# Rows of maxima stored to DRAM in one transfer and loaded in three; queries, features and a value projection of a pass dealt out one step later

## The reference, cut to what matters

```python
mod = (silu(c) @ wmod).reshape(8, 6, 1, 256)          # sa, ca, ga, sb, cb, gb
h = layernorm(x) * (1 + ca) + sa
x = x + ga * attention0(h)      # 16 heads of 16, causal, softmax
h = layernorm(x) * (1 + cb) + sb
x = x + gb * ffn(h)
# ffn(h): xn = layernorm(h) * ln_g + ln_b; o = attention1(xn) + h   (32 heads of 8, not causal)
#         y = gelu(o @ w1[e] + b1[e]) @ w2[e] + b2[e]   with 8 experts, 256 tokens each, chosen by position
```

## Time and profile before

| | |
|---|---|
| median of 3 runs | 1596.53 us (1594.93 to 1596.89) |
| profiled execution | 1600.5 us, its span 1598.7 us |
| TensorE (PE) | busy 1428.8 us, 89% |
| DVE / ACT / POOL | busy 1148.2 us (72%) / 997.1 us (62%) / 485.3 us (30%) |
| mean granted TensorE clock | 0.962 |
| DMA | 203.32 MB, mean 127 GB/s |
| store_max L1016 / load_max L1026 | 288 / 192 issues |
| chain that ended last | PE 65%, DVE 10%, ACT 7%, SPq 6%, DMA 6% |

### The profile page before, as it was taken

One profiled execution on the slowest core, in us unless ns is written; L12 is line 12 of the kernel. 1 busy time (PEld: TensorE's weight loads), 2 busy tenths in 40 slices (PEclk: granted clock), 3 DMA queues, 4 the chain that ended last, 5 costly groups with the idle time before them and its releaser, 6 DMA issues.

```text
span 1598.7 us, 29723 instructions
## 1 busy us (share of the span) xinstructions
PE 1428.8 (89%) x9541; PEld 601.4 (38%) x9541; DVE 1148.2 (72%) x2891; ACT 997.1 (62%) x2075; POOL 485.3 (30%) x1219
## 2 busy tenths in 40 slices
PE   6676578998999989999999989999999989998987
PEld 4222323333344434343343434343343423343426
DVE  6654579868879686878778686878778597867620
ACT  1143256775677766676577766686577766776761
POOL 4122233434333243413333143413233033201000
PEclk9698799999999999999999999999999999999999
DMA  6841434564438273546438263555437342524212
GB/s 189 219 109 29 142 88 112 155 162 130 113 103 232 73 206 88 161 119 181 100 96 234 78 199 95 144 136 169 112 95 203 96 113 72 160 79 106 81 43 66
DMA packets 192734, 203.32 MB, mean 127 GB/s; under 512 B 58048, under 2 KB 143360, under 8 KB 192584
## 3 DMA queue, kind: packets, MB, share of 16 engines
q1 hardware_dynamic: 186696, 197.05, 44.9%
q10 hardware_dynamic: 5888, 4.37, 1.0%
HBM read 123.43 MB, written 77.94 MB: 126 GB/s over the span
## 4 chain that ended last, share of the span: by engine, by line
PE 65%; DVE 10%; ACT 7%; SPq 6%; DMA 6%; issue 4%; POOL 1%; POOLq 0%; ACTq 0%; DVEq 0%
PE bank_out L1471 16%; PE bank_scores L1452 12%; PE bank_max L1430 8%; PE bank_side L1555 7%; PE bank_side L1394 5%; PE bank_side L1404 4%; DVE max_column L1699 3%; PE bank_max L1539 3%; ACT probs L1252 3%; DMA max_rows<-max_parts 2%; PE bank_side L1520 2%; PE bank_side L1509 2%; PE bank_side L1539 2%; SPq L944 2%; SPq L829 2%
## 5 line engine op out<-in xcount | busy, mean ns | idle before, releaser
L1252 ACT ACTIVATE probs<-bank_scores 128x512 f32<-128x512 f32 (+3 forms) x1536 | 752.4, 543 | 333.0 <-PE bank_scores L1452 323.7
L1699 DVE TENSOR_REDUCE max_column<-bank_max 128x1 f32<-128x512 f32 x1024 | 654.3, 684 | 121.8 <-PE bank_max L1430 116.3
L1452 PE MATMUL bank_scores<-q_stack,k_stack 64*128 64x512 bf16 (+3 forms) x2048 | 321.0, 350 | 62.0 <-ACT probs L1252 36.7
L1471 PE MATMUL bank_out<-probs,v_tile 128*9 128x512 f32 (+4 forms) x3072 | 368.4, 552 | 7.8 <-POOL probs L1120 2.9
L1430 PE MATMUL bank_max<-k_stack,q_stack 64*128 64x512 bf16 (+3 forms) x2048 | 319.7, 349 | 49.0 <-DVE max_column L1696 19.1
L1696 DVE CUSTOM_DVE_ANT_0 bank_max<-bank_max,causal 128x384 f32<-128x384 f32 (+3 forms) x512 | 241.7, 515 | 131.2 <-PE bank_max L1430 128.9
L1452 PEld LDWEIGHTS bank_scores<-q_stack,k_stack 64*128 64x128 bf16 x2048 | 81.5, 94 | 442.2 <-issue 409.3
L1102 POOL CAST max_parts<-max_row 128x32 bf16<-128x32 f32 x96 | 23.2, 241 | 456.4 <-DVE max_row L1712 456.4
L1430 PEld LDWEIGHTS bank_max<-k_stack,q_stack 64*128 64x128 bf16 x2048 | 104.2, 95 | 126.7 <-issue 87.0
L1555 PE MATMUL bank_side<-w_out,hidden_T 128*128 128x256 f32 x512 | 141.5, 402 | 3.1 <-issue 1.1
L1120 POOL TENSOR_SCALAR_AFFINE_SELECT probs<-probs 128x512 f32<-128x512 f32 x128 | 81.4, 636 | 97.8 <-ACT probs L1252 97.5
(11 more groups left out here) (153 smaller groups left out, 1361.2 us busy)
## 6 DMA issues: line engine op xcount, KB each, us to landing
q_stack<-q_parts SPq DMA_DIRECT2D x124, 256.0 KB, 4.6
k_stack<-k_parts SPq DMA_DIRECT2D x122, 192.0 KB, 6.2
out_raw<-out_raw SPq DMA_DIRECT2D x70, 256.0 KB, 2.0
w_in<-in_L_ffn_w_dram SPq DMA_DIRECT2D x16, 1024.0 KB, 7.0
w_out<-in_L_ffn_w_dram SPq DMA_DIRECT2D x16, 1024.0 KB, 6.3
q_parts<-partsq SPq DMA_DIRECT2D x32, 384.0 KB, 3.1
k_parts<-partsk SPq DMA_DIRECT2D x32, 384.0 KB, 2.9
q_parts<-partsq SPq DMA_DIRECT2D x32, 256.0 KB, 3.2
```

Source lines behind the costliest of these rows:

```text
L1252: nc.scalar.activation(probs[s % 2][:, head_at(k), q0:S], region[bank][:, q0:S], ACT.Exp, scale=float(WIDTH[a]) ** -0.5).then_inc(drained[ ...
L1452: ins = pe.matmul(region[to][:, q0:S], k_stack[buf][rows, at, kt * P:(kt + 1) * P], q_stack[buf][rows, at, q0:S], start=(i == 0), stop=last)
L1471: ins = pe.matmul(outb[32 * k:32 * k + WIDTH[a] + 1, q0:S], v_tile[a][:, kt, g * GROUP + k, :], probs[s % 2][:, k, q0:S], start=(kt == 0), ...
L1699: v.tensor_reduce(dst, region[bank], AX_X, ALU.max).then_inc(drained[bank], 1)
```

## The change

`max_rows` in DRAM gets another layout, so that the store is a single transfer of 128 rows of 192 bytes, and the load is one transfer for each bf16 part, over both halves of the partitions, whose pieces in DRAM are 64 bytes long (before, two transfers with three rows each). The semaphores' counts follow. `store_max` gets slot 1 instead of 2 of its count, which is slot 2 instead of 3 of the step: the same half, but ahead of what stands in slot 3. In each pass one value projection goes from 61 to 33 and the four attention outputs to 41, 43, 53, 61; the second half of the features, the eight halves of queries and keys, four pieces of the expert output, and store_y, load_expert_out and load_gate go one step later (features 341 and 343 become 343 and 353).

```diff
@@ -50,7 +50,7 @@
 VALUES_SLOT = (3, 1)
 ROWS_AFTER = 1
 BLOCK = 32
-MAX_HOPS = (("max_rows", 0), ("store_max", 2), ("load_max", 4))
+MAX_HOPS = (("max_rows", 0), ("store_max", 1), ("load_max", 4))
 NORMALISE_AFTER = 3
 TURN_SLOT = 1
 NEWTON_PIECE = 3 + GUESS_STEPS
@@ -287,10 +287,10 @@
 
 
     b, e = n + 1, n - 1
-    place_units(plan, first, (3, 13, 61, 63), v_items(0, n + 2))
+    place_units(plan, first, (3, 13, 33, 63), v_items(0, n + 2))
     place_units(plan, first, (13,), [("bias_part", n, 0)])
     place_units(plan, first, (23,), [("head_features", b, 0, 1)])
-    place_units(plan, first, (33, 41, 43, 53), out_items(b))
+    place_units(plan, first, (41, 43, 53, 61), out_items(b))
     place_units(plan, first, (191, 231, 231, 243, 281), heads_items(n, 1, 0))
     place_units(plan, first, (271, 301, 301, 321, 351), heads_items(n + 2, 0, 0))
     place_units(plan, first, (421, 441, 441, 463, 491), heads_items(n, 1, 1))
@@ -318,11 +318,11 @@
     place_cluster(plan, first, 303, e, 1, norm_under(n + 3, 0) if more else ())
     place_units(plan, first, (341,), [("load_expert_in", n, 0)])
     if more:
-        place_units(plan, first, (341, 343), features_items(n + 3, 0))
-        place_units(plan, first, (393, 403, 411, 421, 431, 441, 451, 461), qk_items(0, n + 3))
+        place_units(plan, first, (343, 353), features_items(n + 3, 0))
+        place_units(plan, first, (403, 411, 421, 431, 441, 451, 461, 471), qk_items(0, n + 3))
     place_expert_out(plan, first, (311, 313, 323, 333), e, 1, 0)
-    place_expert_out(plan, first, (353, 363, 373, 383), e, 1, 1)
-    place_units(plan, first, (402, 413, 423), [("store_y", e, 1), ("load_expert_out", n, 0), ("load_gate", n + 1)])
+    place_expert_out(plan, first, (363, 373, 383, 393), e, 1, 1)
+    place_units(plan, first, (412, 423, 433), [("store_y", e, 1), ("load_expert_out", n, 0), ("load_gate", n + 1)])
     place_units(plan, first, (413,), [("keep_v", n + 1)])
     place_units(plan, first, (471,), [("bias_columns", n)])
 
@@ -554,7 +554,7 @@
               nc.dram_tensor("k_parts1", (2, C, SLICES, P, S), BF16, kind="Internal").ap()]
     raw_dram = [nc.dram_tensor("out_raw%d" % a, (HEADS[a] // GROUP, P, S), F32, kind="Internal").ap() for a in range(2)]
     inverse_dram = [nc.dram_tensor("inverse%d" % a, (C, HEADS[a] // C, S), F32, kind="Internal").ap() for a in range(2)]
-    max_dram = nc.dram_tensor("max_rows", (2, M_PARTS, BLOCK, P // BLOCK, BLOCK), BF16, kind="Internal").ap()
+    max_dram = nc.dram_tensor("max_rows", (2, P // BLOCK, BLOCK, M_PARTS, BLOCK), BF16, kind="Internal").ap()
     mod_dram = nc.dram_tensor("mod_rows", (BATCHES, 4 * D), F32, kind="Internal").ap()
 
     with ExitStack() as ctx:
@@ -758,11 +758,11 @@
 
         def rows_sent(b, a, g):
 
-            return 16 * M_PARTS * (HEADS[a] // GROUP // 2 * b + g // 2 + 1)
+            return 16 * (HEADS[a] // GROUP // 2 * b + g // 2 + 1)
 
         def rows_stored(b, a, g):
 
-            return 16 * TILES * (HEADS[a] // GROUP // 2 * b + g // 2 + 1)
+            return M_PARTS * rows_sent(b, a, g)
 
         def chunk_of(a, g):
 
@@ -1011,19 +1011,17 @@
                 ago = groups_ago(b, a, g, 2)
                 if ago:
                     wait(sp, max_stored[ago[1]][g % 2], rows_stored(*ago))
-                for m in range(M_PARTS):
-                    dst = max_dram[g % 2, m].rearrange("c q j -> q c j")
-                    sp.dma_start(dst, max_parts[:, g % 2, m, :]).then_inc(max_sent[a][g % 2], 16)
+                dst = max_dram[g % 2].rearrange("q c m j -> (q c) (m j)")
+                sp.dma_start(dst, max_parts[:, g % 2, :, :].rearrange("p m j -> p (m j)")).then_inc(max_sent[a][g % 2], 16)
 
             def load_max(b, f, a, g):
                 u = unit_of(a, g * GROUP)
                 per, at = GROUP // TILES, column_of(a, g, PASSES[a] - 1, 0)
                 wait(sp, max_sent[a][g % 2], rows_sent(b, a, g))
-                for t in range(TILES):
-                    first = MAX_ROW + t * TILE_ROWS
-                    dst = q_stack[buffer_of(u, b)][first:first + M_PARTS, at:at + per, :]
-                    src = max_dram[g % 2][:, t * per * T:(t + 1) * per * T].rearrange("m (k c) q j -> m k (c q j)", k=per)
-                    sp.dma_start(dst, src).then_inc(max_stored[a][g % 2], 16)
+                for m in range(M_PARTS):
+                    dst = q_stack[buffer_of(u, b)][MAX_ROW + m:P:TILE_ROWS, at:at + per, :]
+                    src = max_dram[g % 2, :, 0:GROUP * T, m, :].rearrange("q c j -> c q j")
+                    sp.dma_start(dst.rearrange("p h (t x) -> p (h t) x", t=T), src).then_inc(max_stored[a][g % 2], 16)
 
             def store_y(b, f, j):
                 wait(sp, y_made, 2 * b + j + 2)
```

## The result

| | median | runs | ratio to the kernel before, 95% interval |
|---|---|---|---|
| before | 1596.89 us | 5 | |
| changed | 1604.70 us | 5 | 1.0047 [1.0027, 1.0068] |
| changed, again, beside the last experiments (before 1601.12) | 1603.70 us | 12 | 1.0016 [0.9997, 1.0036] |

The forecast was 1578, and the range ended at 1591. The first measurement says slower by 0.5%; the second says slower by 0.2%, with an interval that still holds no difference. Both say that there is no gain. The profiled execution of the changed kernel took 1601.74 us (span 1600.0), the fastest of its five, while that of the kernel before was 4 us over its median; so the two profiles, 1.3 us apart, show where the forecast gain is missing, but not where the 0.2 to 0.5% went.

The account below looks back on a forecast made before the run. TensorE, busy 89%, was taken to bound the kernel, its idle time being winnable. Terms −15.8 − 1.6 − 1.5 + 0.5 = −18.4 us gave 1582.1 on the profile's scale, 1578 as a median; range 1572 to 1591.

Parts of the forecast that it names:

- part (2): Maxima's way from SP's store to PE at four pass starts: earlier store, quicker landing end PE's wait; gain 15.8 us.
- the four boundaries: First steps of four later passes, where PE waits 1.76 to 2.20 us for maxima; 15.8 us with low clock.
- A second term of the same sum: Store's start on SP before a pass: 574.9 instead of 576.44, with the second query store behind the load.
- The third term, the load: Load of maxima before a pass: three issues, 1.5 us, then 1.3 us to PE's start.
- The comparison with the 405 boundary: Pass start without the wait takes 9.9 us to the head features, four others 13.7 to 14.1; all should match it.
- Part (1): SP issues: store at 0.4 us, load issues at 0.5; store −1.2 us, load +0.95, SP's total nearly unchanged.
- eight late spots: Places where the maxima's store and load were taken to lie on PE's path: start, first pass, four later pass starts.
- Rival D: Slower: the load's three issues of short pieces are themselves late at pass starts; +10 us, 1606; chance 8%.
- Part (3): Work one step later per pass: steps 34 to 39 gain 1.1 us, 40 to 47 take it; −1.6 us in all.
- rival C: DVE takes over in steps 40 to 48, so PE waits for its maxima; about half the gain left, 1588; 12%.
- Parts (4) and (5): Value projection and attention outputs moved within passes; store of maxima ahead of raw store on SP: both priced at zero.
- Part (6): First pass idle of 1.81 and 1.01 us shrinks, −1.5 us; start, with loads behind stack loads, +0.5 us.

Follow-up runs that it names:

- experiment 10: Changed kernel with only the gate row and bias loads moved behind the boundary's load of maxima: 1599.32 us, 0.9994 against the kernel before.
- experiment 7: Changed kernel with only the 1 MB w_out load moved to step 3 of the next pass: 1580.31 us, 0.9886 against the kernel before.
- experiment 8: Changed kernel with the old layout (three stores, two loads) and w_out load at step 3 of the next pass: 1580.24 us, 0.9890 against the kernel before.
- experiment 1: Kernel before with the new DRAM layout alone (one store, three loads), slots and plan as before: 1607.69 us, ratio 1.0043.
- experiment 6: Kernel before with the load of maxima as three transfers, one per bf16 part, from the old layout; stores as before: 1624.25 us, ratio 1.016.
- experiment 5: Changed kernel with the old layout back, keeping the store's new slot and the moves in each pass: 1591.63 us, 0.9963 against the kernel before.
- experiment 9: Changed kernel measured again, without further edit, beside the last experiments: 1603.70 us, 1.0016 against the kernel before.
- experiment 3: Kernel before with only the store of maxima one slot earlier, ahead of the raw store of the sums: 1597.09 us, ratio 0.9974.
- experiment 11: Kernel before with only the w_out load moved to step 3 of the next pass: 1585.64 us, ratio 0.9900.
- experiment 2: Kernel before with the plan alone (the moves in each pass), stores and loads of maxima as before: 1598.04 us, ratio 0.9983.
- experiment 4: Changed kernel with w_out, gate row and bias loads moved behind the load of maxima: 1602.70 us, 1.0007 against the kernel before.
- experiment 12: Kernel before with new slot, plan, w_out at step 3 of next pass, and batch 1 stack loads later in the start: 1565.75 us, ratio 0.9778.

## Why the prediction was wrong

**The failed step is the landing in part (2): "The store's landing took 3.4 us after its last issue; with one issue and a little less in front I take 2 to 3.4."** From the store's issue to the load the forecast has 2.4 to 3.8 us, and it measured 5.2, 6.0, 5.4 and 5.5 at the four boundaries. I had taken the 3.4 us as a delay counted from the issue. It was the end of a drain: the DMA engines have a share of 1.0 for over 10 us, and this small transfer lands when what was issued before it is through. The view of DMA share in short windows would have shown it in the kernel before; I read the mean of 0.74 over the whole stretch. The store of the earlier trace rows had its last issue at 578.8:

```profile
579.00:580.00 1.00, 0.89 (x10) 0.37 (x8) 0.97 (x3) 0.32 (x2) 1.00 (x2) 1.00 1.09 380
580.00:581.00 1.00, 0.43 (x8) 0.23 (x6) 1.00 (x3) 0.77 (x5) 0.23 (x2) 1.00 0.78 221
581.00:582.00 1.00, 0.89 (x10) 0.17 (x10) 1.00 (x3) 0.00 (x0) 0.56 (x1) 1.00 0.10 14
```

Experiments 10 and 7 show the amount, about 3.4 us for a MB in front. I had even written that w_out moves closer to our store, and gave it no price.

**A second term of the same sum failed with it: "576.44 + 1.3 − 1.0 − 1.8 = 574.9 for our store".** That is 1.5 us sooner than before, against the raw store as a mark; it came 0.5 us sooner at the first boundary and 0.2 in the mean of the four. One reason is seen at the first boundary: behind w_out the issue of the gate row takes 2.20 us instead of 0.43, as much as the query store that left had cost; with w_out gone (experiment 7) it takes 1.15. So the full queue costs twice, in the issues on SP and in the landing. The third term, the load, was sized well: 2.8 us forecast, 2.95 to 3.2 measured. Between the two profiles the forecast was −18.4 us and +1.3 was found; of the 19.7 between them, 15.9 are the boundaries, and 4.1 the tail, which the change doesn't touch (see the end).

**The comparison with the 405 boundary held in its price and failed as a promise.** That a late load costs about 4 us each, half of it as clock, is borne out: experiments 7 and 8 win 3.8 to 4.7 us in each of the four passes, 16.9 and 17.7 us in sum, where the forecast had 15.8 + 1.6. But that boundary has no w_out load in front of it, and its gate row is issued behind the load of maxima (401.30 after 400.68); it was not only the later queries that I named.

**Part (1), the issues.** Sizes right: store 0.34 (forecast 0.4), load 0.49 (0.5). The weight was wrong. "Both lie off PE's path except at the eight late spots": they are not eight. In experiments 1 and 6, which lengthen the load by 0.9 us, PE waits 14 and 17 times instead of 9. Rival D had the right sign and half of the mechanism. The new layout with its longer load does cost, 0.5% between experiments 5 and 9 (0.9963 and 1.0016). But it does so by its third issue and its form, not by short pieces, and only behind a landing that the drain holds back: without w_out (7 and 8) it costs nothing. The packet time of the earlier trace rows holds, though its reading doesn't in one point: the 396 packets are the store's alone, since the load is issued at 590.83, near the end of that window.

**Part (3).** Steps 34 to 39 were to be 1.1 us shorter, "gained in full". They took 0.25 us less, 19.98 us (531.89 to 551.87, from the first scores of step 34 to those of step 40) against 20.23 (535.16 to 555.39); steps 40 to 47, with one piece more, take 26.3 us, before 26.4:

```profile
532.00:552.00 20.00, 19.44 (x146) 6.92 (x144) 15.09 (x53) 13.52 (x25) 0.92 (x4) 1.00 0.43 116
552.00:578.30 26.30, 25.29 (x196) 10.20 (x192) 23.72 (x47) 16.79 (x45) 14.77 (x31) 1.00 0.63 185
```

The idle of steps 40 to 47 hid the moved half, and PE waits for no maxima of DVE in its place, so rival C is out. Why PE did not win the 1.1 us in steps 34 to 39 is open. Up to where PE wants the next pass the two stretches together are 0.34 us shorter, near the forecast of 0.4 a pass; that the sum came out is luck, since the first part fell short. The plan alone gained 2.8 us (forecast 1.6), within its interval.

**Parts (4) and (5).** No run has the moved value projection and outputs by themselves. The slot, priced at zero, gained 4 us (experiment 3). SP no longer holds the store of maxima back behind ACT's copy of the sums, a wait of 396.6 us in all before:

```profile
SPq L721 <- ACT out_raw L1267: 396.6, 53, 20.5
```

It waits for POOL's split instead (559.8 us in experiment 3, 132.9 before). I passed over it because the boundaries I looked at had no such wait directly before the store. At which places the 4 us arise is not shown.

**Part (6).** The start did not get worse by the load: the idle at 105 grew from 6.16 to 6.45 us, the one at 127 shrank from 8.19 to 6.20, and one of 1.09 us came new at 140. Of the two in the first pass, that at 347 is gone, the other went from 1.81 to 1.96 us.

What remains open: why 0.9 us a group costs as much as 25 us in experiment 6 (its 15 us more of idle are seen, and a low clock behind the longer ones, how they arise spot by spot isn't); and why experiment 11 gains 1.0% in time while its profile still shows three waits.

## What to carry to other kernels

In this kernel a small transfer that something waits for landed when the queue in front of it had drained. So where the DMA engines are full, count the bytes ahead of it and read the DMA share around it in windows of one or two microseconds, and don't go by the moment of its issue; then move the large transfers with slack behind it, and behind the next small ones too. When you compare two boundaries, list everything that is issued before each, not only what the change moves. And a transfer split differently trades issues at one end for issues at the other: here those of the load, behind the landing, lay on PE's path at the late places, and those saved on the store bought little there.

## What the runs showed of the hardware

The issue time on SP depended on a transfer's form more than on its pieces: 0.27 us for three adjacent target rows, 0.49 us for two rows 64 partitions apart, with 2 KB runs or with 64 B ones alike, 0.34 us for 128 rows of 192 B in one contiguous target. It also depended on what had been issued before: the issue of the gate row took 0.35 to 0.47 us in the kernel before, and 0.78 to 2.20 us at the five places of the changed one where it stands behind w_out and a key store.

The tail of the kernel (from the last turning of the head features on) is the same work in every version, and in the profiled executions it took 44.3 us in some and 48.3 us in others. What differs in the windows at its start, of the kernel before and of the changed one, is the granted clock:

```profile
1554.40:1560.00 5.60, 4.09 (x12) 1.77 (x12) 0.69 (x1) 2.08 (x3) 0.00 (x0) 1.00 0.01 1
```
```profile
1551.60:1557.00 5.40, 4.69 (x8) 1.89 (x8) 0.00 (x0) 2.08 (x3) 0.00 (x0) 0.50 0.01 2
```

Before both, PE had the same short idle times of 0.7 to 1.2 us between dependent steps. The 4 us came and went with no relation to the edit that I can see (44.3 in experiments 2, 4, 7, 8 and 10, 48.3 to 48.5 in 3, 6, 11 and 12, 46.0, 45.6 and 50.2 in 1, 5 and 9), so two single profiles can differ by that much: the changed kernel's profile was 2.8 us ahead of the other until there.
